# Attention maxima from two-part products in two 32-row tiles of the array, one head in each

## The chip, the cores and the metric

One Trainium2 chip, one of its cores. The time is device time in microseconds (us) of one launch, the median of several runs.

## The reference, cut to what matters

Sixteen sequences of 512 tokens with 128 features go through one layer: attention with 16 heads of 8 elements, a residual and a layer norm, then a top-2 mixture of 8 experts, a residual and a layer norm. All of it is in float32. The change is in the attention's scores:

```
Q = heads(x @ Wq.T + bq); K = heads(x @ Wk.T + bk); V = heads(x @ Wv.T + bv)
scores = einsum('bhqd,bhkd->bhqk', Q, K) / sqrt(8)
probs = softmax(scores, axis=-1)
intervened = probs with key 0 set to 0, divided by max(its sum, 1e-9)
combined = probs + 0.5 * (intervened - probs)
attn_out = einsum('bhqk,bhkd->bhqd', combined, V); out = attn_out @ Wo.T + bo
```

The softmax is stable whatever number near the row's maximum is subtracted before the exponential, since it cancels in the division.

## The kernel before

The float32 queries and keys are split by GpSimd (`split_qk`, L1096) into three bf16 parts each, so that bf16 products on TensorE give float32 accuracy: nine products of parts, each over 8 elements, are stacked in 72 rows of the contraction. The parts are stored to the DRAM tensor `parts_d` (`store_parts`, L316), and `load_qk` (L324) loads them back with copies, so that `QS` and `KS` (four SBUF regions, two for even and two for odd sequences) hold in rows 24a to 24a+23 part a of the queries three times, and beside it the three parts of the keys. The SyncE queue (SP) issues these loads, six for a unit, each of 24 rows of 2048 elements (4 KB).

A unit is four heads of one sequence: 4 units a sequence, 64 in all. For each unit and each of its 8 steps there are three kinds of work, written out by hand in one loop over periods p (from -12) and steps k, the same loop on every engine:

- `maxima(p+2, k)` (PE, L450): two matmuls of 72 x 128 weights on 512 keys, two query chunks of one head, into the two banks of one of two PSUM buffers `mx_ps`. VectorE (DVE, L763) reduces both banks to the negated row maxima. PE may write a buffer again when the reduction two steps back is done.
- `scores(p, 2k)` and `scores(p, 2k+1)` (PE, L465): the transposed scores with the negated maxima added, which are two more rows of the contraction (72 and 73, against rows of ones in `KS`). ScalarE takes the exponential (L632) out of a ring of three PSUM banks.
- `values(p-1, k // 2)` in odd steps (PE, L475): four heads of 32 columns each, in float32, into four column strips of one bank (`acc_ps`).

In step 1 of a period, `negmax_to_rows(p+1)` transposes the maxima of the next unit, ScalarE copies them, GpSimd splits them into two bf16 parts (`split_negmax`, L1086), and SP moves these into rows of `QS` (`move_negmax`, L343), for which the next period's first scores wait. In some steps PE also does projections, transposes and the routing of other sequences (`behind`, L495), listed in `BEHIND` (L240).

SP's order in period p is: move_negmax(p+1), the loads and stores of x, the parts and xT, then load_qk(p+6). Its instructions wait in order. `load_qk` of a sequence's first unit waits until that sequence's parts are stored. Before the first unit of all, loads for four units stand in SP's queue ahead of the transposed input xT of sequence 2, on which PE's projection `q` of that sequence (L499, in period -1) waits. PE and DVE start their work when `s_const` is 6 (L528, L753), of which the last 5 come from GpSimd's memset of `rank` (L1084). After attention come 71 expert tiles and the final norm; they are not touched.

Of the kernel before, what the change touches and what calls it, by code (L numbers as in the profile page):

```python
# [25 lines left out]
P = 128  # L26
NB, L, D = 16, 512, 128
# [4 lines left out]
HG = 4  # L32
NG = NH // HG
VW = 32
PARTS = 3
KR = PARTS * PARTS * DK
MR = 2
E, F = 8, 512
FC = F // P
# [14 lines left out]
def layer(nc, xT, x, wqT, wkT, wvT, woT, bq, bk, bv, bo, gateT, w1T, w3T, w2T, out):  # L54
# [16 lines left out]
    with ctx:  # L71
# [119 lines left out]
        s_const = sem("constants")  # L191
        s_ones, s_const_dve = sem("rows_of_ones"), sem("constants_dve")
        s_pool_const = sem("pool_constant")

        s_xT, s_x = [sem(f"xT_loaded{n}") for n in range(2)], sem("x_loaded")
        s_split, s_split_step = sem("qk_split"), sem("qk_split_step")
        s_parts_stored = [sem(f"{n}_parts_stored") for n in "qk"]
        s_qk_loaded, UNIT_LOADS = [sem(f"qk_loaded{n}") for n in range(2 * NG)], 16 * 2 * PARTS
        s_v_step = sem("values_without_key0")
# [94 lines left out]
        def _(sp):  # L294
# [29 lines left out]
            def load_qk(u):  # L324
                b, g = divmod(u, NG)
                if g == 0:
                    sp.wait_ge(s_parts_stored[0], 16 * (b + 1))
                    sp.wait_ge(s_parts_stored[1], 16 * (b + 1))
                if is_unit(u - 2 * NG):
                    sp.wait_ge(s_ring_ready, ring_at["st", u - 2 * NG, 15] + 1)  # L330
                else:
                    sp.wait_ge(s_ones, 2)
                heads = slice(HG * g * L, HG * (g + 1) * L)
                stored_q, stored_k = (parts_d[b % 2, which][:, :, heads] for which in range(2))
                s_loaded = qk_loaded(u)[0]
                for a in range(PARTS):
                    rows = slice(PARTS * DK * a, PARTS * DK * (a + 1))
                    sp.dma_start(QS[b % 2][rows, HG * g:HG * (g + 1), :],
                                 stored_q[a].unsqueeze(1).to_broadcast([DK, PARTS, HG * L])).then_inc(s_loaded, 16)
                    sp.dma_start(KS[b % 2][rows, HG * g:HG * (g + 1), :],  # L340
                                 stored_k.rearrange("t d q -> d t q")).then_inc(s_loaded, 16)

            def move_negmax(u):  # L343
                b, g = divmod(u, NG)
                sp.wait_ge(s_m_split, u + 1)
                for t in range(MR):
                    sp.dma_start(QS[b % 2][KR + t:KR + t + 1, HG * g:HG * (g + 1), :]
                                 .rearrange("o h (c q) -> o (h c) q", c=QC),
# [92 lines left out]
        def _(pe):  # L441
# [8 lines left out]
            def maxima(u, k):  # L450
# [5 lines left out]
                if k == 0:  # L456
                    pe.wait_ge(*qk_loaded(u))
                h = HG * g + k // 2
                for i in range(2):
                    c = 2 * (k % 2) + i  # L460
                    last = nc.tensor.matmul(mx_ps[n % 2][:, i, :], QS[b % 2][0:KR, h, P * c:P * (c + 1)],  # L461
                                            KS[b % 2][0:KR, h, :], start=True, stop=True)
                last.then_inc(s_mx_ready, 1)

            def scores(u, i):  # L465
# [4 lines left out]
                if i == 0:  # L470
                    pe.wait_ge(s_m_loaded[u % 2], 16 * MR * (u // 2 + 1))
                nc.tensor.matmul(bank, KS[b % 2][0:KR + MR, h, P * c:P * (c + 1)],  # L472
                                 QS[b % 2][0:KR + MR, h, :], start=True, stop=True).then_inc(s_ring_ready, 1)

# [266 lines left out]
        def _(dve):  # L741
# [21 lines left out]
            def maxima(u, k):  # L763

                n = STEPS * u + k
                if k == 0 and u >= 2:
                    dve.wait_ge(s_ring_ready, ring_at["mT", u - 2] + 1)
                dve.wait_ge(s_mx_ready, n + 1)
                V.tensor_reduce(rowmax[u % 2][:, 2 * k:2 * k + 2], mx_ps[n % 2][:, :, :], axis=AXX, op=ALU.max,  # L769
                                negate=True).then_inc(s_mx_done, 1)  # L770
# [283 lines left out]
        def _(pool):  # L1054
# [27 lines left out]
            cst(G.memset(padrow[:, :], 0.0))  # L1082
            cst(G.memset(padrow[:, D:D + 1].bitcast(i32), SKIP))
            G.memset(rank[:, :], 0.0).then_inc(s_const, 5)  # L1084

# [238 lines left out]
```

## Time and profile before

| | |
|---|---|
| median of 3 runs | 1364.8 us (1364.0 to 1367.9) |
| the profiled execution's own time | 1357.14 us |
| its span | 1355.4 us |
| mean granted clock of TensorE | 0.981 of full |
| busy over the span | PE 94%, DVE 69%, ACT 61%, POOL 54% |
| attention, whole | from about 34 to 890 us |
| experts and final norm | from about 890 us on |

Busy time counts an engine as busy while an instruction is in it; matmuls overlap in it, so a busy PE may still stand in a gap between two streams. The start of a matmul is told well by the trace, its end is modelled. PEld is the load of weights. The number of a line (L461) is its line in the kernel before.

### The profile page before, as it was taken

What the parts mean: (1) busy time and instruction counts of PE and PEld (TensorE: products, weight loads), DVE (VectorE), ACT (ScalarE), POOL (GpSimd) and SP (SyncE); (2) the same over time, 40 slices, a digit from 0 to 9 for tenths busy, and PEclk for the clock granted to TensorE, in tenths of its full rate; (3) what the DMA queues carried; (4) which work ended last, traced back from release to release, by engine and by line L of the source; (5) the groups of instructions that cost most, each with busy time, mean ns of one, the idle gap of its engine ahead of it and who ended that gap; (6) DMA issues with size and microseconds to landing.
All of it is one profiled execution on the core that took longest, in us unless ns stands there. A gap on an engine that the chain in (4) does not pass through costs nothing.

```text
span 1355.4 us, 22134 instructions
## 1 busy us (share of the span) xinstructions
PE 1272.2 (94%) x7214; PEld 657.1 (48%) x7214; DVE 941.3 (69%) x1560; ACT 822.7 (61%) x1587; POOL 725.4 (54%) x913
## 2 busy tenths in 40 slices
PE   2799999999999999999999999998899999999967
PEld 1133333333333333333333333257789999999942
DVE  6788898898899898988988999833533333333324
ACT  1277777777777777777777777763434444444416
POOL 4324254474474564654644733546775555555547
PEclk8699999999999999999999999999999999999979
DMA  3322323233323323233232231443344333333327
GB/s 102 121 87 67 94 70 98 80 94 93 95 82 94 109 71 105 84 94 91 88 97 81 84 95 33 152 131 54 59 73 69 53 51 48 48 49 46 43 94 279
DMA packets 111888, 117.18 MB, mean 86 GB/s; under 512 B 17440, under 2 KB 91680, under 8 KB 111392
## 3 DMA queue, kind: packets, MB, share of 16 engines
q1 hardware_dynamic: 86960, 97.62, 23.5%
q0 software_dynamic: 24816, 18.15, 9.2%
q8 instruction: 60, 0.98, 0.3%
q14 instruction: 52, 0.43, 0.1%
HBM read 70.81 MB, written 45.29 MB: 86 GB/s over the span
## 4 chain that ended last, share of the span: by engine, by line
PE 72%; DVE 16%; issue 4%; POOL 3%; DMA 2%; ACT 1%; SPq 1%; another core or an unknown queue 0%; POOLq 0%; ACTq 0%; DVEq 0%
PE acc_ps L484 15%; PE ring_ps L472 13%; PE mx_ps L461 12%; DVE rowmax_sb L769 10%; PE ring_ps L585 8%; PE mx_ps L569 8%; PE mx_ps L560 8%; PE ring_ps L504 1%; PE ring_ps L501 1%; PE ring_ps L499 1%; PE ring_ps L509 1%; POOL x_d L1272 1%; PE ring_ps L518 1%; PE ring_ps L550 1%; DVE TN_sb L778 1%
## 5 line engine op out<-in xcount | busy, mean ns | idle before, releaser
L769 DVE TENSOR_REDUCE rowmax_sb<-mx_ps 128x2 f32<-128x1024 f32 x512 | 607.0, 1213 | 88.3 <-PE mx_ps L461 82.9
L635 ACT ACTIVATE probs_sb<-ring_ps 128x512 f32<-128x512 f32 x1024 | 558.7, 598 | 103.9 <-PE ring_ps L472 88.8
L472 PE MATMUL ring_ps<-region_sb 74*128 74x512 bf16 x1024 | 356.8, 381 | 3.7 <-ACT prefix_sb L671 2.1
L461 PE MATMUL mx_ps<-region_sb 72*128 72x512 bf16 x1024 | 310.3, 385 | 11.1 <-DVE rowmax_sb L769 5.2
L484 PE MATMUL acc_ps<-probs_sb,values_sb 128*32 128x512 f32 x2048 | 272.6, 605 | 5.4 <-DVE TN_sb L778 5.4
L472 PEld LDWEIGHTS ring_ps<-region_sb 74*128 74x128 bf16 x1024 | 100.9, 99 | 234.7 <-ACT probs_sb L635 131.8
L702 ACT ACTIVATE xT_sb<-region_sb 128x512 f32 x71 | 44.8, 630 | 207.4 <-PE mx_ps L569 187.8
L1091 POOL CAST negmax_parts_sb<-negmax_sb 16x128 bf16<-16x128 f32 x64 | 17.9, 280 | 274.9 <-ACT negmax_sb L641 274.9
L1272 POOL DMA_INDIRECT x_d<-probs_sb,values_sb x72 | 111.9, 1554 | 87.4 <-DVE probs_sb L1031 66.5
L461 PEld LDWEIGHTS mx_ps<-region_sb 72*128 72x128 bf16 x1024 | 95.7, 99 | 123.7 <-DVE rowmax_sb L769 36.1
L1031 DVE TENSOR_SCALAR probs_sb<-ring_ps,values_sb 128x128 f32<-128x128 f32 x142 | 43.2, 346 | 159.6 <-PE ring_ps L585 146.0
L1196 POOL DMA_INDIRECT rows_d<-sent_sb,pos_sb x128 | 126.2, 986 | 48.4 <-issue 43.7
L585 PE MATMUL ring_ps<-region_sb,probs_sb 128*128 x1136 | 139.4, 276 | 10.1 <-DVE probs_sb L1037 9.9
L1272 POOL DMA_INDIRECT y_d<-probs_sb,values_sb x70 | 108.7, 1553 | 72.9 <-DVE probs_sb L1031 59.8
L1037 DVE TENSOR_TENSOR probs_sb<-mx_ps,probs_sb 128x1024 f32<-128x1024 f32 x71 | 86.9, 1224 | 79.9 <-PE mx_ps L569 76.1
L560 PE MATMUL mx_ps<-k_parts_sb,xT_sb 128*128 128x256 f32 x568 | 135.9, 383 | 2.8 <-issue 2.8
L585 PEld LDWEIGHTS ring_ps<-region_sb,probs_sb 128*128 128x128 f32 x1136 | 132.4, 192 | 12.6 <-issue 12.4
L560 PEld LDWEIGHTS mx_ps<-k_parts_sb,xT_sb 128*128 128x128 f32 x568 | 108.3, 191 | 18.6 <-issue 3.9
L484 PEld LDWEIGHTS acc_ps<-probs_sb,values_sb 128*32 128x32 f32 x2048 | 40.5, 108 | 113.3 <-issue 94.4
L721 ACT ACTIVATE probs_sb<-mx_ps 128x1024 f32<-128x1024 f32 x71 | 72.6, 1022 | 9.2 <-PE mx_ps L560 6.6
L569 PE MATMUL mx_ps<-k_parts_sb,full_q_sb 128*128 128x256 f32 x288 | 68.1, 379 | 0.0
L569 PE MATMUL mx_ps<-k_parts_sb,full_k_sb 128*128 128x256 f32 x280 | 66.2, 379 | 0.0
(150 smaller groups left out, 1206.0 us busy)
## 6 DMA issues: line engine op xcount, KB each, us to landing
region_sb<-parts_d SPq DMA_DIRECT2D x384, 96.0 KB
values_sb<-rows_d SPq DMA_DIRECT2D x71, 132.0 KB
parts_d<-q_parts_sb SPq DMA_DIRECT2D x16, 384.0 KB, 2.6
parts_d<-k_parts_sb SPq DMA_DIRECT2D x16, 384.0 KB, 2.9
xT_sb<-xT SPq DMA_DIRECT2D x16, 256.0 KB, 3.1
x_sb<-x SPq DMA_DIRECT2D x16, 256.0 KB
x_d<-xn_sb SPq DMA_DIRECT2D x16, 256.0 KB
y_d<-padrow_sb SPq DMA_DIRECT2D x16, 256.0 KB
```

What stands on the lines that cost most here:

```text
L461: last = nc.tensor.matmul(mx_ps[n % 2][:, i, :], QS[b % 2][0:KR, h, P * c:P * (c + 1)], KS[b % 2][0:KR, h, :], start=True, stop=True)
L472: nc.tensor.matmul(bank, KS[b % 2][0:KR + MR, h, P * c:P * (c + 1)], QS[b % 2][0:KR + MR, h, :], start=True, stop=True).then_inc(s_ring_re ...
L484: last = nc.tensor.matmul(acc_ps[VW * j:VW * (j + 1), 0, :], VE[b % 2][:, c, HG * g + j, :], PT[u % 2][:, j, c, :], start=(c == 0), stop=( ...
L560: last = nc.tensor.matmul(up_ps[:, c, :], W1T[t % 2][:, P * c:P * (c + 1)], XGT[t % 2], start=True, stop=True)
L569: last = nc.tensor.matmul(lin_ps[:, c, :], W3T[t % 2][:, P * c:P * (c + 1)], XGT[t % 2], start=True, stop=True)
L585: last = nc.tensor.matmul(y_ps[:, at:at + D], HH[t % 2][:, c, P * w:P * (w + 1)], W2[:, bass.ds(expert + c * D, D)], start=(c == 0), stop= ...
L635: nc.scalar.activation(PT[u % 2][:, i // QC, i % QC, :], ring_bank("st", u, i), ACT.Exp, scale=SCALE).then_inc(s_ring_done, 1)
L721: nc.scalar.activation(SG[t % 2], up_ps, ACT.Silu).then_inc(s_silu, 1)
L769: V.tensor_reduce(rowmax[u % 2][:, 2 * k:2 * k + 2], mx_ps[n % 2][:, :, :], axis=AXX, op=ALU.max, negate=True).then_inc(s_mx_done, 1)
L1037: V.tensor_tensor(HH[t % 2], lin_ps, SG[t % 2], ALU.mult).then_inc(s_h, 1)
L1196: G.indirect_dma_start(rows_d, bass.IndirectOffsetOnAxis(ap=pos[b % 2][:, s, c:c + 1], axis=0), XE[b % 2][:, c, s, :], None).then_inc(s_sc ...
L1272: G.indirect_dma_start((x1_d, y_d)[t % 2], bass.IndirectOffsetOnAxis(ap=XG[t % RING][:, w, D:D + 1].bitcast(i32), axis=0), YO[t % YRING][: ...
```

## The change

The maxima are now taken over four products only: the first two parts of the queries by the first two of the keys, 32 rows. They stand in rows 0 to 31 for a unit's first two heads and in rows 96 to 127 for its last two. A step's two matmuls are then of two different heads, each on its own 32 rows, for one query chunk. The scores still use all nine products: the five others stand in rows 54 to 93 and the maxima in rows 94 and 95, so that the first two heads use rows 0 to 95 and the last two rows 0 to 127. What lies between must be zero, so GpSimd first clears rows 0 to 63 of the four regions. A unit is loaded by ten DMAs, where it was six, with the same bytes (576 KB).

```
-KR = PARTS * PARTS * DK
+TWO = MR * MR * DK
+REST = 54
+NEGMAX = REST + (PARTS * PARTS - MR * MR) * DK
```

In `load_qk` (TWO is 32, NEGMAX is 94):

```
                     sp.wait_ge(s_ones, 2)
+                    sp.wait_ge(s_zeros, 2 * (b % 2) + 2)
-                for a in range(PARTS):
-                    rows = slice(PARTS * DK * a, PARTS * DK * (a + 1))
-                    sp.dma_start(QS[b % 2][rows, HG * g:HG * (g + 1), :],
-                                 stored_q[a].unsqueeze(1).to_broadcast([DK, PARTS, HG * L])).then_inc(s_loaded, 16)
-                    sp.dma_start(KS[b % 2][rows, HG * g:HG * (g + 1), :],
-                                 stored_k.rearrange("t d q -> d t q")).then_inc(s_loaded, 16)
+                for n, row in enumerate((0, P - TWO)):
+                    half = slice(HG * g + HG // 2 * n, HG * g + HG // 2 * (n + 1))
+                    cols = slice(HG * L // 2 * n, HG * L // 2 * (n + 1))
+                    for a in range(MR):
+                        rows = slice(row + MR * DK * a, row + MR * DK * (a + 1))
+                        sp.dma_start(QS[b % 2][rows, half, :], stored_q[a, :, cols].unsqueeze(0)
+                                     .to_broadcast([MR, DK, HG * L // 2])).then_inc(s_loaded, 16)
+                    sp.dma_start(KS[b % 2][row:row + TWO, half, :],
+                                 stored_k[0:MR, :, cols].rearrange("t d q -> (t d) q").unsqueeze(0)
+                                 .to_broadcast([MR, MR * DK, HG * L // 2])).then_inc(s_loaded, 16)
+                unit, mid = slice(HG * g, HG * (g + 1)), REST + MR * DK
+                sp.dma_start(QS[b % 2][REST:mid, unit, :], stored_q[0:MR]).then_inc(s_loaded, 16)
+                sp.dma_start(KS[b % 2][REST:mid, unit, :],
+                             stored_k[MR].unsqueeze(0).to_broadcast([MR, DK, HG * L])).then_inc(s_loaded, 16)
+                sp.dma_start(QS[b % 2][mid:NEGMAX, unit, :],
+                             stored_q[MR].unsqueeze(0).to_broadcast([PARTS, DK, HG * L])).then_inc(s_loaded, 16)
+                sp.dma_start(KS[b % 2][mid:NEGMAX, unit, :], stored_k).then_inc(s_loaded, 16)
```

In `maxima` of PE, and then in `scores`:

```
+                c = k % QC
+                for i, row in enumerate((0, P - TWO)):
+                    h = HG * g + HG // 2 * i + k // QC
+                    last = nc.tensor.matmul(mx_ps[n % 2][:, i, :], QS[b % 2][row:row + TWO, h, P * c:P * (c + 1)],
+                                            KS[b % 2][row:row + TWO, h, :], start=True, stop=True)
...
+                rows = slice(0, P if h % HG >= HG // 2 else P - TWO)
+                nc.tensor.matmul(bank, KS[b % 2][rows, h, P * c:P * (c + 1)],
+                                 QS[b % 2][rows, h, :], start=True, stop=True).then_inc(s_ring_ready, 1)
```

DVE's reduction stays as it is but for the places of its two results in `rowmax`. Among GpSimd's constants, ahead of the memset of `rank`:

```
+            for n in (0, 2, 1, 3):
+                G.memset(regions[n][0:64, :], 0.0).then_inc(s_zeros, 1)
```

## Rows read from the trace of the kernel before

**Rows 1.** The page: busy time by engine; the chain that ended last, by engine.
```profile
PE 1272.2 (94%) x7214; PEld 657.1 (48%) x7214; DVE 941.3 (69%) x1560; ACT 822.7 (61%) x1587; POOL 725.4 (54%) x913
...
PE 72%; DVE 16%; issue 4%; POOL 3%; DMA 2%; ACT 1%; SPq 1%; another core or an unknown queue 0%; POOLq 0%; ACTq 0%; DVEq 0%
```
**Rows 2.** Windows, four periods of one sequence: from:to length, busy (instructions) by engine, PEclk, DMA share, GB/s.
```profile
396.50:409.00 12.50, 12.14 (x72) 4.19 (x70) 11.34 (x19) 9.17 (x19) 10.50 (x14) 1.00 0.22 71
409.00:422.90 13.90, 13.80 (x78) 5.03 (x78) 11.35 (x14) 10.16 (x21) 2.63 (x7) 1.00 0.41 123
422.90:435.50 12.60, 12.25 (x70) 3.80 (x69) 12.16 (x24) 9.06 (x19) 7.72 (x10) 1.00 0.31 88
435.50:449.40 13.90, 13.90 (x81) 4.93 (x79) 12.75 (x21) 10.33 (x21) 8.76 (x15) 1.00 0.25 80
sum 52.90, PE 52.10 PEld 17.94 DVE 47.59 ACT 38.72 POOL 29.61; mean PE 13.02 PEld 4.49 DVE 11.90 ACT 9.68 POOL 7.40
```
**Rows 3.** Timeline of PE, two steps of a period: start, length, engine, line, operation.
```profile
404.91 0.39 PE L472 MATMUL ring_ps<-region_sb 74*128 74x512 bf16 x1
405.14 0.60 PE L461 MATMUL mx_ps<-region_sb 72*128 72x512 bf16 x2
...
406.01 0.60 PE L461 MATMUL mx_ps<-region_sb 72*128 72x512 bf16 x2
406.44 0.38 PE L472 MATMUL ring_ps<-region_sb 74*128 74x512 bf16 x1
406.75 1.07 PE L484 MATMUL acc_ps<-probs_sb,values_sb 128*32 128x512 f32 x8
407.75 0.39 PE L472 MATMUL ring_ps<-region_sb 74*128 74x512 bf16 x1
```
**Rows 4.** Timeline of PEld, the weight load after the values.
```profile
404.91 0.10 PEld L472 LDWEIGHTS ring_ps<-region_sb 74*128 74x128 bf16 x1 [0.84 <-ACT probs_sb L635]
```
**Rows 5.** Timeline of PE, float32 matmuls with bf16 ones behind them.
```profile
410.96 1.02 PE L499 MATMUL ring_ps<-xT_sb,wq_sb 128*128 128x512 f32 x2
411.82 0.38 PE L472 MATMUL ring_ps<-region_sb 74*128 74x512 bf16 x1
```
**Rows 6.** Timeline of DVE from 60 to 66 us.
```profile
59.89 6.87 DVE L769 TENSOR_REDUCE rowmax_sb<-mx_ps 128x2 f32<-128x1024 f32 x6
```
**Rows 7.** Timeline of GpSimd's last constants.
```profile
3.80 0.21 POOL L1082 MEMSET padrow_sb<- 128x132 f32 x1
...
4.29 0.10 POOL L1084 MEMSET rank_sb<- 128x4 f32 x1
```
**Rows 8.** Timeline of PE at the start, with its idle time before.
```profile
14.18 2.05 PE L499 MATMUL ring_ps<-xT_sb,wq_sb 128*128 128x512 f32 x2 [14.18 <-ACT wo_half_sb L625]
...
59.22 0.38 PE L472 MATMUL ring_ps<-region_sb 74*128 74x512 bf16 x1
```
**Rows 9.** The chain that ended last, 24 to 62 us: start, length, what.
```profile
30.95 3.30 DMA region_sb<-parts_d
...
45.16 4.47 DMA xT_sb<-xT
...
49.76 2.05 PE ring_ps L499 x2
```
**Rows 10.** Timeline of SP's queue at the start.
```profile
27.40 0.70 SPq L338 DMA_DIRECT2D region_sb<-parts_d  x1
...
40.00 0.44 SPq L321 DMA_DIRECT2D parts_d<-q_parts_sb  x1
...
53.29 1.22 SPq L347 DMA_DIRECT2D region_sb<-negmax_parts_sb  x2
```
**Rows 11.** Windows with loads of a unit, with stores, and of the final stage; columns of rows 2.
```profile
35.00:38.00 3.00, 1.51 (x6) 0.23 (x4) 2.98 (x3) 0.00 (x0) 2.78 (x4) 1.00 0.46 145
46.00:47.00 1.00, 0.00 (x0) 0.00 (x0) 0.69 (x1) 0.00 (x0) 0.70 (x2) 0.50 0.99 298
...
1316.00:1318.00 2.00, 2.00 (x3) 0.67 (x2) 1.17 (x8) 0.00 (x0) 0.00 (x1) 0.50 1.03 390
```

More of the change, by code:

```diff
@@ L192, in layer @@
         s_ones, s_const_dve = sem("rows_of_ones"), sem("constants_dve")
+        s_zeros = sem("rows_of_zeros")
         s_pool_const = sem("pool_constant")
@@ L197, in layer @@
         s_parts_stored = [sem(f"{n}_parts_stored") for n in "qk"]
-        s_qk_loaded, UNIT_LOADS = [sem(f"qk_loaded{n}") for n in range(2 * NG)], 16 * 2 * PARTS
+        s_qk_loaded, UNIT_LOADS = [sem(f"qk_loaded{n}") for n in range(2 * NG)], 16 * 10
         s_v_step = sem("values_without_key0")
@@ L346, in move_negmax @@
                 for t in range(MR):
-                    sp.dma_start(QS[b % 2][KR + t:KR + t + 1, HG * g:HG * (g + 1), :]
+                    sp.dma_start(QS[b % 2][NEGMAX + t:NEGMAX + t + 1, HG * g:HG * (g + 1), :]
                                  .rearrange("o h (c q) -> o (h c) q", c=QC),
@@ L457, in maxima @@
                     pe.wait_ge(*qk_loaded(u))
[L458 to L462, printed above, removed]
+                c = k % QC
[3 more added lines that the diff above has]
+                                            KS[b % 2][row:row + TWO, h, :], start=True, stop=True)
                 last.then_inc(s_mx_ready, 1)
@@ L471, in scores @@
                     pe.wait_ge(s_m_loaded[u % 2], 16 * MR * (u // 2 + 1))
-                nc.tensor.matmul(bank, KS[b % 2][0:KR + MR, h, P * c:P * (c + 1)],
-                                 QS[b % 2][0:KR + MR, h, :], start=True, stop=True).then_inc(s_ring_ready, 1)
+                rows = slice(0, P if h % HG >= HG // 2 else P - TWO)
+                nc.tensor.matmul(bank, KS[b % 2][rows, h, P * c:P * (c + 1)],
+                                 QS[b % 2][rows, h, :], start=True, stop=True).then_inc(s_ring_ready, 1)
             def values(u, c):
@@ L768, in maxima @@
                 dve.wait_ge(s_mx_ready, n + 1)
-                V.tensor_reduce(rowmax[u % 2][:, 2 * k:2 * k + 2], mx_ps[n % 2][:, :, :], axis=AXX, op=ALU.max,
+                by_head = rowmax[u % 2][:, :].rearrange("p (i a c) -> p i a c", i=2, c=QC)
+                V.tensor_reduce(by_head[:, :, k // QC, k % QC], mx_ps[n % 2][:, :, :], axis=AXX, op=ALU.max,
                                 negate=True).then_inc(s_mx_done, 1)
```

## The prediction

> **What bounds the kernel now.** I read the page first. PE is busy 94% of the span, and the chain that ended last runs on PE for 72% and on DVE for 16% [rows 1]. The windows give the steady state: one sequence takes 52.9 us, in which PE is busy 52.1 and DVE 47.6 [rows 2]. So PE bounds attention, and DVE stands only 10% behind it. The maxima's matmuls are two of the four bf16 ones of a step, which makes this the right place to look, but a large gain would soon meet DVE.
>
> The timeline of PE then shows what a step is made of [rows 3]. A bf16 matmul of 512 columns takes 0.22 us from start to start: the pair of maxima starts at 406.01, the scores behind it at 406.44, so the pair costs 0.43. The values, four abreast in column strips, are different at both edges. They start 0.31 after the scores (406.44 to 406.75), 0.09 later than a matmul of the same kind would. They are eight, four at a time, in two passes. Two float32 matmuls of 512 columns take 0.86 (410.96 to 411.82 [rows 5]); the values take 1.00 (406.75 to 407.75 [rows 3]). Of the 0.14 above it, some 0.03 are loading 32 columns twice as long as bf16 and 0.02 the stagger of the four, and 0.09 is again a gap before the full-width matmul. It isn't the data type: between float32 and bf16 at full width there is no gap [rows 5]. It isn't ScalarE either, to which the trace gives the 0.84 [rows 4]: it recurs at 0.09 wherever values end. So PE lets one arrangement of the array run dry before it begins another, 0.09 us each way, and 0.01 more because the next weights could not be loaded in advance (404.91 to 405.14 is 0.23, where 0.22 is usual).
>
> The Trainium skill states this as a rule ("TensorEngine Tiling (Array Packing)", Key Properties): changing the tiling mode, and not merely the tile, drains the engine. By that rule the trace agrees for column strips; no row here shows row tiles.
>
> **The change part by part.**
>
> 1. *The maxima's pair.* Before: 0.43. After: the two run side by side, 0.22 with 0.01 of stagger, but between matmuls of another arrangement, scores before and scores behind. That is 0.09 in, 0.01 for the weights, 0.22 for both, 0.09 out and 0.01 for the weights of the scores: 0.42 to 0.43. What the pair gains (0.21) its two edges take (0.20). Sum for 64 x 8 = 512 steps: 0. From both sides: if row tiles need no edge, -0.20 a step, which DVE cuts short (below); if each of the two weight loads is exposed in full (0.10 [rows 4]), +0.20 a step, 512 x 0.20 = +102. I take 0, because the values' edges are the nearest rows, the same engine and the same neighbours. The results reach DVE about 0.1 earlier in a step, which is worth nothing while PE bounds. The scores' 96 or 128 rows instead of 74 change no column count: 0.
>
> 2. *DVE's reduction.* Same input, 128x1024, two results: 1.13 us back to back (six take 6.87, of which the last 0.08 overlaps [rows 6]): 0.
>
> 3. *Four memsets on GpSimd* of 64 rows by 4096 float32, ahead of the memset of rank which releases PE. 132 elements take 0.21 us and 4 take 0.10 [rows 7], 0.86 ns an element, so 3.5 us each and 14.1 in all. rank would end at 18.5 in place of 4.4. PE begins now at 14.18, held by the weights' DMAs through ScalarE [rows 8], so 14.18 - 4.4 = 9.8 of it is hidden: **+4.3 us** at the start. DVE waits for the same release, and has nothing to reduce before the first unit is loaded.
>
> 4. *Ten loads a unit instead of six.* SP issues 18 of the old ones in 12.6 us (27.40 to 40.00 [rows 10]), 0.70 each. I take 0.70 for the eight new ones of the same broadcast form and 0.48 (a store is issued in 0.44 [rows 10]) for the two that are plain copies: 6.6 us a unit against 4.2. In the steady state SP has 13.2 us a period and needs 6.6 + 1.2 (the move of the maxima [rows 10]) and now and then a store, and a unit is loaded six periods ahead: hidden. The move of the maxima can be late by the longer loads, 2.4 us, but it is issued in the first half of a period and needed in the next. If that cover fell, it would be up to 2.4 us once a sequence, 38 in all. At the start it isn't hidden: four units stand ahead of xT in the queue, 4 x 2.4 = **9.5 us**.
>
> 5. *How many DMA engines carry them.* While old units are loaded, the DMA share is 0.46 at most, 7.4 of 16 engines; with stores under way it is 0.99 [rows 11]. The old loads have a leading dimension of 8, the stores 128. I infer that a transfer is divided along its leading dimension. Six of the new loads of a unit have 2 or 3 in front (the copies are made by a leading broadcast): the four of the halves' queries, the two of the halves' keys; and so have the third part of the keys (2) and of the queries (3). Then the first engine carries 4 x 16 + 2 x 32 + 32 + 32 KB of these, and of the two plain copies 4 + 8: 204 KB, or 209 thousand bytes. An engine moves 390 / (1.03 x 16) = 23.7 GB/s [rows 11]: 8.8 us a unit. The other traffic (91 GB/s in all [rows 2] less the loads' 45, over 16 engines) adds 1.6: in the steady state 10.4 of 13.2 us, hidden. At the start, four units queue on that engine: the first flows at about 27.4 + 4.3 + 1.5 = 33.2; three units end at 59.6, the store of the queries' parts takes 1.3, unit 3 ends at 69.7, the second store at 71.0, and xT lands at 72.0. Now it lands at 49.63 [rows 9]. **+22.4 us**, which contains parts 3 and 4. From there PE has 59.22 - 49.76 = 9.5 us of work until the first scores [rows 8, 9]: 81.6. Unit 4's loads and the maxima behind them (issued at 53.29 now [rows 10]) would land at 82.3. So the first scores come at 82.3, not 59.22: **+23 us**, and nothing gives that back, since PE bounds from there on. Bounds: +13.8 (parts 3 and 4 alone, the engines no limit) and +35 (an engine at 19 GB/s, as the page's mean would have it). I take 23, by the rows of saturated engines.
>
> The Trainium skill ("DMA: Bandwidth & Descriptors", why a DMA increments its semaphore by 16) gives the number of engines as the largest number up to 16 that divides the slowest dimension of both sides: 8 before, 2 and 3 now. By it the sum is the same as mine.
>
> **Sum:** 1357.1 (the profiled execution) + 23 + 0 = 1380. The median of the runs lies 7.7 above the profiled execution (1364.8 - 1357.1), so **1388 us**.
>
> **The rivals.**
>
> - *A: row tiles run without the edges.* For it: the edges that the trace shows are all those of column strips. Then PE needs 52.9 - 32 x 0.20 = 46.5 us a sequence and DVE 47.6. The two wait for each other, since `mx_ps` has two buffers only and DVE's other work comes in lumps: I take 50. The gain is 16 x 2.9 = 46, less the 23 of the start: 1342. If only one of two edges falls away, about 1350. This is the faster side, and it decides as soon as a pair costs less than 0.38 (0.05 x 512 is more than the start's 23). The Trainium skill ("TensorE: Matmul & The Clock Gate", Measured speedup) gives four row tiles together 3.07 times the speed of one after the other, which speaks for the pair, not for its edges.
> - *B: edges as forecast, but the loads are spread over eight engines or more.* +13.8: 1379.
> - *C: tiles dearer than the values' edges* (weight loads one after the other, or the pair not side by side): +0.1 a step is 51 us: 1439; one after the other entirely (+0.22) 1500. Against it: the values' four start within 0.02.
> - *D: two DMA engines become the bound.* This needs more than 13.2 us a unit, so the plain copies on two engines as well (256 KB) and 19 GB/s: 13.8 + 1.5. 64 x 2.1 more, and a longer start: about 1540.
> - *E: PE's clock falls* from full (2.4 GHz) in rows 2 to half (1.2 GHz), as in the row at 46 us, where PE has stood idle [rows 11]. Against it: PE still streams three quarters of its time. Over 1500.
>
> **How the numbers follow.** Forecast 0.45, A 0.25, B 0.12, C 0.10, D 0.06, E 0.02. The likeliest case has 1376 to 1404 for itself. The range takes in A from 1333 and C up to 1430. No change means within 0.3%, 1361 to 1369, about what the runs can tell: only A half way falls there, 0.04. Faster is the rest of A, 0.22; slower 0.74.
>
> **What would show it.** Scores to maxima 0.31 from start to start, the pair within 0.02, maxima to scores 0.32; under rival A 0.22 and 0.23. Four memsets of 3.5 us on GpSimd, PE's first matmul at 18.5. First scores near 82 us (59 now). A sequence in the steady state 52.9 within 0.5. DMA share while units are loaded near 0.15, not 0.45. The forecast is wrong if a sequence takes under 51 us or over 54, or if the first scores come before 70.

## The result and the profile after

| | before | after |
|---|---|---|
| median of 15 runs | 1362.47 us (1351.16 to 1367.90) | 1371.76 us (1370.66 to 1374.82) |
| ratio, 95% interval | | 1.0085 (1.0066 to 1.0104) |
| profiled execution, its span | 1357.14, 1355.4 us | 1371.96, 1370.2 us |
| first scores | 59.22 us | 82.57 us |
| first accumulator drained by DVE | 81.9 us | 109.8 us |
| the same of unit 56 | 817.6 us | 836.4 us |
| last one; from it to the end | 900.9; 454.5 us | 916.0; 454.3 us |

The milestones in the lower rows are from the two profiled executions. An accumulator is the bank `acc_ps` of one unit, and DVE drains it with one transpose, of which there are 64.

The kernel is slower, as forecast, but by 9.3 us between the medians (about 12 by the ratio), where 23 were forecast. The milestones split the 14.8 us between the two spans: 27.9 lost before the first accumulator, 12.8 regained from there to the last, 0.2 behind it.

The page of the kernel after, busy time and chain by engine (beside [rows 1]):

```profile
PE 1265.6 (92%) x7214; PEld 610.0 (45%) x7214; DVE 938.6 (69%) x1560; ACT 822.7 (60%) x1587; POOL 739.1 (54%) x917
...
PE 73%; DVE 14%; POOL 4%; issue 3%; SPq 3%; DMA 2%; ACT 1%; POOLq 0%; ACTq 0%; DVEq 0%
```

Windows of one sequence in the changed kernel, with the columns of [rows 2]:

```profile
422.00:434.30 12.30, 12.02 (x73) 3.49 (x71) 11.17 (x18) 9.11 (x19) 10.44 (x15) 1.00 0.29 93
434.30:448.10 13.80, 13.77 (x78) 4.51 (x77) 11.32 (x14) 10.20 (x21) 2.71 (x7) 1.00 0.40 63
448.10:460.70 12.60, 12.34 (x72) 3.16 (x72) 12.21 (x23) 9.23 (x19) 7.69 (x10) 1.00 0.48 126
460.70:474.00 13.30, 13.30 (x79) 3.79 (x77) 12.49 (x20) 10.12 (x20) 8.71 (x14) 1.00 0.44 90
sum 52.00, PE 51.43 PEld 14.95 DVE 47.20 ACT 38.65 POOL 29.55; mean PE 12.86 PEld 3.74 DVE 11.80 ACT 9.66 POOL 7.39
```

A sequence takes 52.0 us, not 52.9. From here on "cycle" is the median distance between DVE's transposes of the same unit in two successive sequences: 52.81 us in the kernel before and 52.03 in the changed one. An "edge" is a change of the array's arrangement, between matmuls on full rows and matmuls in tiles. The timeline of PE (start, length) shows two steps with their edges:

```profile
417.76 0.39 PE L492 MATMUL ring_ps<-region_sb 128*128 128x512 bf16 x1
418.08 0.39 PE L480 MATMUL mx_ps<-region_sb 32*128 32x512 bf16 x2
418.40 0.61 PE L492 MATMUL ring_ps<-region_sb 128*128 128x512 bf16 x2
418.94 0.39 PE L480 MATMUL mx_ps<-region_sb 32*128 32x512 bf16 x2
419.26 0.39 PE L492 MATMUL ring_ps<-region_sb 128*128 128x512 bf16 x1
419.58 1.07 PE L504 MATMUL acc_ps<-probs_sb,values_sb 128*32 128x512 f32 x8
420.58 0.39 PE L492 MATMUL ring_ps<-region_sb 96*128 96x512 bf16 x1
```

Scores to maxima is 0.32 and maxima to scores 0.32 in these rows; the medians of the starts from 200 to 840 us are 0.314 and 0.317. The two of a pair start 3 ns apart. Two steps, from values to values, take 2.82 us, and 2.84 in the kernel before.

The start: GpSimd's timeline, the last rows of SP's queue ahead of the first scores, and the chain.

```profile
4.23 13.85 POOL L1106 MEMSET region_sb<- 64x4096 f32 x4
18.02 0.09 POOL L1107 MEMSET rank_sb<- 128x4 f32 x1
...
51.01 2.57 SPq L348 DMA_DIRECT2D region_sb<-parts_d  x2
...
60.84 1.02 SPq L304 DMA_DIRECT2D xT_sb<-xT  x1
```

```profile
60.40 10.51 DMA parts_d<-k_parts_sb
...
78.39 4.04 DMA region_sb<-negmax_parts_sb
82.57 0.58 PE ring_ps L492
```

PE's first matmul starts at 18.21. xT is issued at 60.84 and lands 10.7 later (4.5 before [rows 9]). But the chain that ends at the first scores does not go through xT. It goes through SP's queue: the store of the keys' parts takes 10.5 us to land (4.3 in the kernel before), then SP issues the ten loads of unit 4, and only then, at 77.73, the move of the first unit's maxima, which GpSimd had ready at 55.5. PE waits 2.3 us for that move, so the way through xT has that much slack.

SP's issuing itself also slows: three units of ten loads take about 6.3 us each, the fourth 9.3, with two pairs of query loads at 2.57 (above) and 3.04 us in place of 1.3.

The first window below lies just behind the first scores of the changed kernel, and the second is the same stretch of the kernel before, behind its own first scores:

```profile
84.00:94.00 10.00, 10.00 (x29) 1.64 (x27) 8.17 (x7) 7.14 (x14) 4.16 (x6) 0.50 0.26 65
```

```profile
62.00:72.00 10.00, 9.36 (x42) 2.67 (x42) 10.00 (x10) 9.32 (x18) 4.17 (x6) 1.00 0.21 61
```

PE was at half clock (1.2 GHz) until about 100 us, with 29 matmul records in 10 us against 42 at full (2.4 GHz). From the first scores to the first accumulator it took 27.3 us, and 22.6 in the kernel before.

### The profile page after: what moved, and what is told of

It is laid out like the page before. It is cut to its first block, busy times and chain, and to the rows that moved or that the text cites. A ratio compares the mean times of both kernels' runs of the same rounds, so it can differ in the third digit from the quotient of the medians.

```text
span 1370.2 us, 22401 instructions
## 1 busy us (share of the span) xinstructions
PE 1265.6 (92%) x7214; PEld 610.0 (45%) x7214; DVE 938.6 (69%) x1560; ACT 822.7 (60%) x1587; POOL 739.1 (54%) x917
## 4 chain that ended last, share of the span: by engine, by line
PE 73%; DVE 14%; POOL 4%; issue 3%; SPq 3%; DMA 2%; ACT 1%; POOLq 0%; ACTq 0%; DVEq 0%
PE ring_ps L492 15%; PE acc_ps L504 15%; PE mx_ps L480 9%; PE ring_ps L605 9%; DVE rowmax_sb L790 8%; PE mx_ps L589 8%; PE mx_ps L580 8%; PE mx_ps L637 1%; DVE TN_sb L799 1%; PE ring_ps L524 1%; SPq L348 1%; PE ring_ps L538 1%; PE ring_ps L570 1%; POOL region_sb L1106 1%; PE ring_ps L529 1%
## 5 line engine op out<-in xcount | busy, mean ns | idle before, releaser
L492 PE MATMUL ring_ps<-region_sb 96*128 96x512 bf16 (+1 forms) x1024 | 365.1, 391 | 3.9 <-DMA region_sb<-negmax_parts_sb 2.3
L480 PE MATMUL mx_ps<-region_sb 32*128 32x512 bf16 x1024 | 204.0, 396 | 18.4 <-DVE rowmax_sb L790 9.2
L492 PEld LDWEIGHTS ring_ps<-region_sb 96*128 96x128 bf16 (+1 forms) x1024 | 86.8, 99 | 258.1 <-ACT probs_sb L655 147.2
L480 PEld LDWEIGHTS mx_ps<-region_sb 32*128 32x128 bf16 x1024 | 48.1, 91 | 202.1 <-issue 116.1
```

Of the source, the lines that this page charges most:

```text
L480: last = nc.tensor.matmul(mx_ps[n % 2][:, i, :], QS[b % 2][row:row + TWO, h, P * c:P * (c + 1)], KS[b % 2][row:row + TWO, h, :], start=Tru ...
L492: nc.tensor.matmul(bank, KS[b % 2][rows, h, P * c:P * (c + 1)], QS[b % 2][rows, h, :], start=True, stop=True).then_inc(s_ring_ready, 1)
```

## The experiments

Every kernel ran on a chip with the kernel before beside it. The medians of the kernel before are 1357.1 to 1360.8 us on three of the chips and 1374.2 on the fourth. So ratios to the kernel before are compared, and milestones of the profiled executions. Even a ratio carries about 1% from chip to chip (e3_both and e3_again below are the same kernel); that of the changed kernel was the same twice, 1.0085 and 1.0084.

### The start: GpSimd and the number of engines

**e1_zero_late.** Among the constants `rank` comes first; regions 1 and 3 are cleared after the first sequence's splits.

```
-            for n in (0, 2, 1, 3):
-                G.memset(regions[n][0:64, :], 0.0).then_inc(s_zeros, 1)
             G.memset(rank[:, :], 0.0).then_inc(s_const, 5)
+            for n in (0, 2): ...
```

> The changed kernel, but rank's memset comes before the clearing of the regions, and the two regions of odd sequences are cleared only after the first splits. Theory (the start costs 23 us, of which the memsets ahead of rank are 4.1, hidden by nothing): PE starts at 14.2 in place of 18.2, all of the start moves up by 4.1, first scores at 78.5 in place of 82.6, the run 4.1 below the changed kernel, about 1368. Rival (the queue of the two loading DMA engines alone sets the start, and the memsets only fill its shadow): first scores stay near 82.5, the run near 1372.

1363.96 us, ratio 1.0047 (1.0020 to 1.0073). PE began at 11.46, the first scores came at 76.05, the first accumulator at 103.5: 6.3 less than in the changed kernel. The direction is the theory's, but PE began 2.7 us earlier than the 14.2 of the kernel before. The last of the weights let ScalarE start at 11.05 here and at 13.77 there. Here GpSimd issues its own writes of `rows_d` at 11.24, there at 4.91, while SP is still issuing the weights. That these writes delay the weights is argued, not shown.

**e2_eight.** The same ten loads, each with a leading dimension of 8 or 16.

```
-  QS[rows, half] <- stored_q[a, :, cols].unsqueeze(0).to_broadcast([MR, DK, ..])
+  QS[rows, half] <- stored_q[0:MR, :, cols].rearrange("a d q -> d a q")
-  KS[row:row + TWO, half] <- "(t d) q" .unsqueeze(0).to_broadcast([MR, MR * DK, ..])
+  KS[row:row + TWO, half] <- "(t d) q" .unsqueeze(1).to_broadcast([MR * DK, MR, ..])
```

> The changed kernel with the same ten loads of the same bytes a unit, but the copies ordered so that every source has 8 or 16 in front. Theory (a transfer is divided along its leading dimension, and the two engines' queue delays xT): xT of sequence 2 lands at 64 to 65 us in place of 71.5, first scores near 75, the run 7 to 8 below the changed kernel, about 1364. DMA share while units are loaded near 0.45. Rival (SP's issue of ten loads a unit is what delays it): xT lands at 71 as before, the run at 1372.

1362.32 us, ratio 1.0021 (1.0002 to 1.0039). SP issues xT at 60.0, much as in the changed kernel (60.8), but it lands after 3.9 us in place of 10.7:

```profile
DMA to landing us min/median/max: 3.9/3.9/3.9
```

First scores at 73.18, 9.4 earlier; cycle 52.03, as in the changed kernel. The same bytes and the same number of loads with another leading dimension moved them. The DMA share from 31 to 60 us rose only from 0.26 to 0.32, where 0.45 was expected, which fits SP's issuing as what sets the pace now (e12). That a transfer is divided by its leading dimension is what the Trainium skill states in "DMA: Bandwidth & Descriptors" (why a DMA increments its semaphore by 16) of the slowest dimension; the trace agrees with its direction (10.7 and 3.9 us), and no row here counts the engines of one transfer.

**e3_both** and, on another chip, **e3_again**: both edits together.

> The changed kernel with both repairs of its start at once: rank is cleared ahead of the four regions, two of which are cleared later, and the ten loads of a unit are led by 8 or 16. Alone the first repair brought the first scores from 82.6 to 76.1 us and the second to 73.2, in the profiled executions. Theory (the start is a sum of a late PE and of transfers on few engines, and nothing of it is made good later): first scores near 67 us, the cycle of a sequence unchanged at 52.0, the time 12 to 16 us below the changed kernel, near 1357 to 1360. Rival (they share one wait, so the second repair brings nothing once the first is made): first scores at 73 or later, the time near 1362 again. Second question: the granted clock. If PE is held at half by the 32-row matmuls of the start, it still rises only some 15 us after the first scores and these are 27 us ahead of the first accumulator transposes; if the pause of PE before the first scores did it, 23 us.

> The changed kernel with both repairs of its start, once more, beside the others. Theory: without single waits strewn over it the cycle is 52.03, first scores at 66 to 67, and the ratio to the kernel before is 0.999 to 1.001: 16 us of start given back, of which the clock takes some, since the first accumulator transpose comes 27 to 30 us behind the first scores. Rival (the strewn waits belong to these loads, led by 8 or 16 and more in number of packets, and not to the chip): cycles of 52 to 56 us again and a ratio of 1.006.

First scores at 66.07 and 66.14: the two gains (6.5 and 9.4) add up, 16.5 together. The first run had single sequences of 51.1 to 55.9 us and a ratio of 1.0067 (1.0043 to 1.0092). These are its waits of PE from 200 to 840 us (us in total, times, longest):

```profile
PE ring_ps L531 <- ACT negmax_sb L663: 8.0, 8, 1.2
...
PE ring_ps L494 <- ACT prefix_sb L693: 3.8, 7, 0.8
```

The second had a cycle of 52.03 and a ratio of 0.9975 (0.9947 to 1.0004). So these waits, which I call strewn, belong to that chip or hour and not to the loads; the kernel before also took 1374.2 us there. What causes them is open. Without them the changed kernel with its start repaired can't be told from the kernel before; with them it is slower.

In both runs the first scores wait for the move of the maxima behind unit 4's ten loads, as in the changed kernel. To issue that move ahead of these loads is the obvious next experiment at the start; it was not run.

**f1_before_zero.** The kernel before with the four memsets alone (into the buffers of the probabilities).

```
+            for n in range(4):
+                G.memset(pt_flat[n % 2][0:64, ...], 0.0).then_inc(s_zeros, 1)
             G.memset(rank[:, :], 0.0).then_inc(s_const, 5)
```

> The kernel before with only the four memsets of the change added (64 x 4096 float32 each, here into the buffers of the probabilities, ahead of rank on GpSimd). Theory: PE's first matmul goes from about 14.2 to 18.2 us, the first scores from 59.2 to about 63, the time is 3 to 5 us more than before: 1.0025 to 1.004. Rival (the start has slack, since the loads of parts wait for SP and not for PE): 0, a ratio of 1.000. The clock rises at the first scores as in the kernel before, since the maxima still take 72 rows: 22.7 us from the first scores to the first accumulator transpose. Were it 27, the late start and not the 32-row matmuls would be the cause of the late clock.

PE at 18.23, first scores at 64.41, first accumulator 22.5 behind them. Ratio 1.0025 (0.9987 to 1.0064), on the chip with the strewn waits: the total alone doesn't separate it from 0, the milestones do (+5.0 at the first accumulator). So the memsets cost 5 us of the 27.9, and PE's later start alone does not delay the clock: it is at full from about 65 us.

### The clock

**e4_one_tile.** Both matmuls of a pair on rows 0 to 31, one after the other, heads of the first half; the maxima of a unit's last two heads are left out.

```
-                for i, row in enumerate((0, P - TWO)):
-                    h = HG * g + HG // 2 * i + k // QC
+                for i, row in enumerate((0, 0)):
+                    h = HG * g + k // QC
```

> The changed kernel with both matmuls of the maxima's pair on rows 0 to 31 (both take the first two heads; the maxima of the last two heads are left out and theirs are used instead). Theory (the two run side by side, and the gain of that is eaten by two gaps of 0.09 to 0.10): the pair grows by 0.21 us a step, PE bounds, 512 steps give +108, about 1480. Rival (the pair's own time never was the limit, DVE's reduction is): a few us, 1372 to 1385.

One run, 1463.45 us, so 92 above the changed kernel's median where 108 were expected; cycle 57.70, so 5.67 or 0.177 a step on average for not running side by side. In the plain steps, where PE alone bounds, it is 0.21:

```profile
417.69 0.61 PE L492 MATMUL ring_ps<-region_sb 96*128 96x512 bf16 x2
418.23 0.60 PE L480 MATMUL mx_ps<-region_sb 32*128 32x512 bf16 x2
418.76 0.39 PE L492 MATMUL ring_ps<-region_sb 96*128 96x512 bf16 x1
```

From the maxima to the scores behind them it is 0.53 here and 0.32 in the changed kernel. Its window behind the first scores:

```profile
84.00:94.00 10.00, 9.64 (x22) 1.51 (x23) 6.19 (x6) 5.58 (x11) 4.17 (x6) 0.50 0.27 61
```

PE streams one matmul after the other and the clock is still at half, until about 111 us. So it isn't that the pair leaves PE idle; what is left is that these matmuls use 32 rows in a tile, where the kernel before used 72.

**e7_full_rows.** The pair on rows 0 to 93, full width, everything else as changed; the last two heads' maxima lack four products.

```
-  QS[b % 2][row:row + TWO, h, ..], KS[b % 2][row:row + TWO, h, :]
+  QS[b % 2][0:NEGMAX, h, ..],      KS[b % 2][0:NEGMAX, h, :]
```

> The changed kernel with both matmuls of a maxima pair on rows 0 to 93, one arrangement for all bf16 work, so no tiles of the array; heads, loads, memsets and DVE's work stay. The maxima of the first two heads of a unit then have all nine products and those of the last two lack four. It separates what the row tiles do from what the rest of the change does. Theory (the pair gains 0.21 and its edges take 0.20, so the steady state hardly depends on it): the cycle goes back from 52.0 to 52.8 us, since DVE gets the maxima as late as before; first scores as in the changed kernel near 82, but PE's clock is at full from there and the first accumulator transpose follows after 23 us in place of 27. In sum -4.6 at the start, +12 over 15 sequences: 7 to 8 us above the changed kernel. Rival (what the changed kernel regained per sequence came from the new order of heads or the loads, not from the tiles): cycle 52.0 again and the time 4 to 5 us below the changed kernel. A second rival (32-row matmuls don't hold the clock down, the pause ahead of the first scores does): 27 us again.

```profile
84.00:94.00 10.00, 9.29 (x40) 2.74 (x39) 9.40 (x9) 9.14 (x18) 4.17 (x6) 0.95 0.28 69
```

The clock is near full behind the first scores (80.95), and the first accumulator follows after 22.9 us. The cycle is 52.59. 1375.61 us, ratio 1.0111 (1.0060 to 1.0163), 5.1 above the changed kernel beside it (**after_again**: 1370.52 us, ratio 1.0084, 1.0055 to 1.0114, cycle 52.03). The theory's direction holds on both counts; its 7 to 8 was too much. The two ratios overlap, so the cycles and the milestones carry this. The edit changes the number of rows and takes away the tiles at once, so no run here says which of the two holds the clock down.

> The changed kernel once more, on the same chip as the three others, because runs of the kernel before differ by 1% between chips and by 1% from run to run. Theory (the changed kernel costs 23 to 28 us at the start and regains 12 in the steady state): a ratio of 1.008 to 1.011 to the kernel before on whatever chip, cycle 52.0. Rival (on a chip where single waits of 0.2 to 1 us are strewn over the steady state, the kernel with the shorter step loses more): a ratio above 1.012.

**e8_filler.** As e3_both, with nine float32 matmuls of 128 rows whose results are thrown away.

```
+                    if (p == -1 and k > 0) or (p == 0 and k < 2):
+                        nc.tensor.matmul(acc_ps[:, 0, :], wq_sb[:, :], xT_sb[1][:, :], start=True, stop=True)
```

> As the kernel with both repairs of the start, with nine float32 matmuls of 512 columns more (128 rows, results thrown away) on PE, one in each step from the second of the period ahead of the first scores to the second step of the first period of scores. Theory (the clock stays at half over the first scores because PE streams too little ahead of them through 32 rows): the clock is at full near the first scores, the first accumulator transpose comes 23 us behind the first scores and not 27, and the time is 2 to 4 us below the kernel with both repairs. Rival (the clock of this stretch costs nothing, since ScalarE, DVE or the loads bound it): 27 us again and the time the same or 1 to 3 us more, for the added matmuls.

```profile
60.00:70.00 10.00, 10.00 (x26) 2.94 (x26) 6.34 (x6) 0.69 (x1) 0.00 (x0) 0.87 0.24 67
```

The clock is at full from about 63 us, so at the first scores (70.65). The first accumulator comes 22.6 behind them, in e3_both beside it 29.8. But the fillers cost 4.6 ahead of the scores: net 2.6 (93.3 for 95.8). Ratio 1.0038 (1.0000 to 1.0075) against 1.0067: the intervals overlap.

### What is left of the start

**e9_all.** e3_both, xT issued one period earlier, and in odd steps scores, scores, maxima, values.

> As the kernel with both repairs of the start, with xT issued one period earlier in SP's queue and odd steps in the order scores, scores, maxima, values. Theory: the first scores come near 63 us since xT no longer stands behind the last unit's loads, the cycle is 51.8, the time 4 to 7 us below the kernel with both repairs, near 1353, which would be below the kernel before. Rival (xT is late for another reason, such as the copies of x ahead of it): first scores as in the kernel with both repairs, and 3 us from the cycle alone.

xT now lands at 49.8 (56.5 in e3_both), and yet the first scores come at 66.53: the rival's outcome. The chain says why: SP moves the maxima at 63.86, behind unit 4's ten loads, and xT was not what the first scores waited for. Ratio 1.0067 (1.0031 to 1.0103), with strewn waits (single sequences up to 60.9 us): nothing can be read from its total.

**f2_before_queues**, **e12_queues.** Units 1 and 3 are issued by ScalarE, in the kernel before and in the one that groups the maxima (below).

```
-                if is_unit(p + 6):
+                if is_unit(p + 6) and p + 6 not in (1, 3):
...
+                if p == -5:
+                    load_qk(act, 1)
+                    load_qk(act, 3)
```

> The kernel before with only one edit: of the four units loaded ahead of xT, the second and the fourth are issued by ScalarE, which has nothing to do there, and no longer by SP. Theory (at the start SP's issuing, 0.70 us a load, is what xT waits for): 12 loads leave SP's queue, 8.4 us; xT lands near 41 instead of 49.6, the first scores near 51 to 54 instead of 59.2, the time 5 to 8 us below the kernel before, a ratio of 0.994 to 0.996. Rival (the start is bound by PE's and DVE's work on the first units): first scores at 58 to 59, ratio 1.000.

> The kernel with the maxima of two steps together and both repairs of the start, and with the loads of the second and the fourth unit issued by ScalarE. Theory (10 loads of 0.70 us a unit in SP's queue are what is left of the late start): 20 loads, 14 us, leave SP's queue; two units fewer ahead of xT: first scores near 55 to 57 us (66.7 without), the time 9 to 12 us below that kernel, a ratio of 0.990 to 0.992 to the kernel before. Rival (something else bounds, such as the memsets on GpSimd ahead of the second sequence's parts): first scores at 64 or later, ratio 0.997 to 0.999.

In the kernel before xT is now issued at 38.68, but the chain shows it landing where it did:

```profile
38.68 10.32 DMA xT_sb<-xT
```

First scores at 58.34 (59.22 before): the rival. The ratio, 0.9974 (0.9941 to 1.0006), would allow either. xT and the store of the keys' parts are issued about 6.4 us earlier, but they take 10.3 and 10.1 us to land (4.5 and 4.3 before), so SP moves the first maxima at 52.67 (53.29 before). In the one that groups the maxima ScalarE's issues brought the first scores from 66.71 to 54.75 (expected 55 to 57), since SP's move of the maxima comes at 51.97 and not at 63.65. The ratio went from 0.9983 to 0.9898 (0.9838 to 0.9958), on another chip. There xT took:

```profile
DMA to landing us min/median/max: 5.7/5.7/5.7
```

So with ten loads a unit, once they are spread, SP's issuing at about 0.7 us each bounds the start; with six of the old form it doesn't alone.

### The steady state

**e5_beside_values.** In odd steps scores, scores, maxima, values: one change of arrangement fewer in two steps.

```
+                    if is_unit(p) and k % 2 == 1:
+                        scores(p, 2 * k + 1)
                     if is_unit(p + 2):
                         maxima(p + 2, k)
-                    if is_unit(p):
+                    if is_unit(p) and k % 2 == 0:
```

> The changed kernel with the maxima of odd steps issued behind the step's second scores, next to the values. Two steps then have five changes of the array's arrangement where they had six. Theory (each change costs PE 0.10 and PE bounds): 256 x 0.10 = 26 us less, about 1346, somewhat less where DVE gets its maxima 0.2 later. Rival (DVE bounds by now, PE's gaps are slack): no gain or a loss, 1370 to 1380.

1365.46 us, ratio 1.0042 (1.0023 to 1.0061), so about 6 us less where 26 were expected; cycle 51.83, 0.2 less. The fastest pairs of steps took 2.72 (for 2.82), as priced, but as many took 2.78 or 2.82, and one period of the four grew from 13.81 to 14.07. Three scores now stand one behind the other, and ScalarE has three banks: the scores' weight loads wait for it for 172.7 us between 100 and 800 us, in the changed kernel for 117.0. That this took the rest back is argued.

**e10_two_steps.** The maxima of two steps together, behind the scores of the even one; 4 changes of arrangement in two steps in place of 6.

```
                     if is_unit(p):
                         scores(p, 2 * k)
+                        scores(p, 2 * k + 1)
-                    if is_unit(p + 2):
+                    if is_unit(p + 2) and k % 2 == 0:
                         maxima(p + 2, k)
+                        maxima(p + 2, k + 1)
```

> The changed kernel with the maxima of two steps issued together: even steps are scores, scores, both maxima pairs; odd steps scores, scores, values. Nothing else changes. In two steps the array then changes its arrangement 4 times where it did 6 times. Theory (an edge costs 0.09 to 0.10 us and the rest streams): two steps of 5.6 us in all are shorter by 0.2, 16 of these in a sequence: 3.2 us less, cycle 48.8, if DVE (47.6 busy in a sequence) follows; I expect 49 to 50, the time 30 to 45 us below the changed kernel, 1325 to 1340. Rival (DVE's two reductions of 1.13 one behind the other and its lumps of other work make PE wait for a buffer of the maxima, since both are filled at once): cycle 51 to 53, the time within 15 us of the changed kernel. Third (no edge cost at all between matmuls of row tiles and full rows: the distances of 0.31 have another cause): the distances scores to maxima stay at 0.31 but the cycle does not move though DVE waits.

1372.31 us, ratio 1.0104 (1.0053 to 1.0156), cycle 52.46, where 49 to 50 were expected.

```profile
409.01 1.06 PE L504 MATMUL acc_ps<-probs_sb,values_sb 128*32 128x512 f32 x8
410.01 0.60 PE L492 MATMUL ring_ps<-region_sb 128*128 128x512 bf16 x2
410.55 0.60 PE L480 MATMUL mx_ps<-region_sb 32*128 32x512 bf16 x4
411.08 0.60 PE L492 MATMUL ring_ps<-region_sb 128*128 128x512 bf16 x2
411.62 1.06 PE L504 MATMUL acc_ps<-probs_sb,values_sb 128*32 128x512 f32 x8
```

The plain two steps take 2.61 us, 0.21 less, which is two edges of 0.106. The waits of PE from 200 to 840 us show who took it back. In the changed kernel the first row is 3.0 us (6.2 in after_again) and the last 3.9:

```profile
PE mx_ps L480 <- DVE rowmax_sb L790: 37.9, 63, 1.2
...
PE acc_ps L504 <- DVE TN_sb L799: 3.7, 13, 0.3
```

The rival: both buffers are filled at once, and each lump of DVE's other work makes PE wait.

**e11_two_steps_start.** The same with e3_both's start.

> As the kernel with the maxima of two steps together, and both repairs of the start (two of the regions cleared later and rank ahead of all; loads led by 8 or 16). Theory: first scores near 66 us in place of 82, 12 to 14 us below the kernel without the repairs, since nothing of the start is made good; 1315 to 1325 where the kernel before takes 1360, so faster than both. Rival (where DVE bounds, a start lost or won changes less): 5 us or less between the two.

1355.96 us, ratio 0.9983 (0.9955 to 1.0011), 16.3 below e10. The rival falls: the start comes back in full. The 1315 to 1325 of the theory took e10's expected gain as given.

**e13_mixed.** As e12, grouped only in the periods with g = 3 and through the first period of scores.

```
+                    pairs = g == 3 or p < 1
```

> As the last, but the maxima of two steps are issued together only in every fourth period (g = 3) and up to the first scores; elsewhere they are spread as in the changed kernel. By the periods of the two kernels measured (12.32, 13.81, 12.58, 13.33 spread and 12.80, 13.40, 12.88, 13.41 grouped) only the second of these gains by grouping. Theory (periods are independent, DVE's lumps decide in each): a cycle of 51.6 us (52.03 less 0.41), 12 us less over 15 sequences than the grouped kernel's 52.47. Rival (DVE carries its lateness from one period into the next, so the gain of one is lost in the next): a cycle of 52.0.

1336.58 us (1335.41 to 1342.32), **ratio 0.9857 (0.9793 to 0.9920)**, cycle 51.62: the theory's cycle to 0.02. The total fell by 7.8 us against e12 where 12 were expected, partly since the first sequence, 46.3 us in e12, takes 48.4 here. PE's wait over the same stretch:

```profile
PE mx_ps L482 <- DVE rowmax_sb L800: 7.7, 27, 0.6
```

This version beats the kernel before by 24 us on the same chip, and e3_again beside it by 19. The changed kernel itself did not run on that chip.

## Why the prediction was right or wrong

The forecast was a change of 23 us between the medians; it was 9.3. The first scores were as late as forecast (23.4 for 23). Missed were 12.8 us regained in the steady state, 4.6 lost to the clock behind the first scores, and the distance of the base.

**The pair: the term that was mis-sized.** "Sum for 64 x 8 = 512 steps: 0" measured -12.8 us, 0.025 a step. The mechanism stands: in at 0.31, out at 0.32, the pair side by side, where three distances of 0.22 stood before. e10 and e5 price an edge at 0.10 by taking edges away, so what the values showed for column strips holds for row tiles too. The Trainium skill's "TensorEngine Tiling (Array Packing)", Key Properties, says it of any change of the tiling mode, and the trace now agrees for both kinds (0.106 an edge in e10). But 0.314 + 0.003 + 0.317 is 0.634 where three distances were 0.654, and scores to scores and scores to values give half of that gain back (0.227 for 0.219, 0.320 for 0.309). In hundredths this was nothing; over the 256 pairs of steps it is 4 to 5 us.

The rest was not in the plain steps: the sequence has 16 two-step blocks, 0.02 each is 0.3, while e7, equal but for the tiles and their rows, shows 0.56 (52.59 to 52.03). I wrote that results reaching DVE 0.1 earlier are "worth nothing while PE bounds"; the period where DVE transposes and takes reciprocals lost 0.26 in that comparison (13.59 to 13.33). That DVE's head start is the cause is argued, not shown; the sums of waits can't settle it, since the changed kernel and after_again list 6.9 and 16.0 us of PE's waits at the same cycle. The remaining 0.2 a sequence lies in single waits of the profiled kernel before, among them 2.1 us for `prefix` in 620 us; f2, whose steady state is the same code, shows 52.60. So about a quarter of the 12.8 is the one execution of the kernel before that was profiled. The profiled execution of the changed kernel lost something too: one sequence took 53.58 us, with the clock at half around 213 to 216 us, where after_again has 52.04.

**The start: right**, in its path too: the 82.3 was unit 4's loads with the maxima behind them in SP's queue, and so was the 82.57. First scores at 82.57 for 82.3, memsets 13.85 us for 14.1, PE at 18.21 for 18.5, xT for 72.0 landed at 71.5, an issue of ten loads 6.3 for 6.6. The DMA share from 31 to 60 us was 0.26 where 0.15 was forecast for the loading of units. Both causes are shown one by one (e1 6.5, e2 9.4 of the first scores' time, together 16.5). That 7 were left against the kernel before had its reason in SP's issuing (e12). Of e1's 6.5, 2.7 are weights that came earlier than in the kernel before, not a memset taken back.

**The clock: a rival with the wrong place.** Rival E asked whether PE falls to half in the steady state. It didn't. But at the start it stayed at half 17 us beyond the first scores, which cost 4.6 us (27.3 for 22.6). No term of the sum had it. e4, e7, e8 and f1 show the cause: the maxima's matmuls in 32-row tiles, neither the idle time nor the late start. Whether it is their rows or the tiles is open. The rows of the prediction had a half clock at 46 us, and I let the 72-row maxima's recovery stand for the new ones.

**The base.** The sum was 1380 and I added 7.7, what the median of 3 runs lay above the profiled execution. The kernel after has no such distance (1371.96 and 1371.76). Over 15 runs the distance of the kernel before is 5.3 (1362.47), so the 14.8 between the profiled executions become 9.3 between the medians. Against the forecast: start +4.9 (27.9 for 23), steady state -12.8, base -7.7, behind attention and rounding -0.6: 1388 - 16.2 = 1371.8. The kernel before scatters over 17 us from run to run, the changed one over 4. The granted clock goes with it. Of 16 runs of the kernel before beside after_again, six had a mean clock of 0.979 to 0.981 and took 1351.5 to 1356.0 us, ten had 0.970 to 0.976 and took 1357.7 to 1367.4. Its profiled execution had 0.981, and the changed kernel had 0.970 at most in 15 runs. So the prediction read its trace from an execution with a higher clock than most. What sets the clock of an execution, no run here tells.

**The other rivals.** A fell: no edge fell away. B was the changed kernel with e2's edit: its first scores came 14.0 us later than in the kernel before, where 13.8 were priced, but the time was 1362 and not 1379, by the same terms that failed the sum. C's "one after the other" is what e4 shows, 0.21 in a plain step as priced (0.22) but 0.177 on average. D didn't happen: loads cost nothing in the steady state, by e2's equal cycle.

## What to carry to other kernels

A tile mode that gains one matmul's time pays that back at its two edges when it serves one pair. Group the pairs, but only as far as the buffers behind them let the next engine smooth its own lumps (here in one period of four). Keep thousandths where a step recurs 512 times. Before adding transfers, look at what the start waits for: the same ten loads were free in the steady state, and ahead of the first scores they cost the larger part of 23 us, by their leading dimension and by the queue that issued them; a memset in front of a release cost the rest. Before trusting one execution as the base, compare its mean clock with those of the other runs.

## What the runs showed of the hardware that was not expected

- TensorE's granted clock stayed at half with matmuls of 32 rows in tiles even while PE's records fill 96% of the window (e4, 0.50 from 84 to 94 us), and was near full in the same place with 94 rows and no tiles (e7, 0.95).
- A change between full rows and row tiles costs 0.10 us (two of them 0.21 in e10), as much as with column strips (0.09 [rows 3]); the second matmul of a pair starts 3 ns after the first.
- An x transfer of 256 KB took 3.9 (e2), 4.5 (the kernel before), 5.7 (e12), 10.3 (f2) or 10.7 us (the changed kernel) from issue to landing, beside other traffic each time.
- On one chip most sequences of a kernel took 0.4 to 2.4 us more in single waits (e3_both); on another the same kernel stayed at 52.03 (e3_again).
